# Attention's begin and the quantised FFN: order of splits, scores and product parts; one pass less in each rounding

## The reference, cut to what matters

```python
q2 = (q @ wiq.T + biq).reshape(N, H, D).transpose(1, 0, 2)      # N 384, H 16 heads, D 64
k2 = (k @ wik.T + bik).reshape(N, H, D).transpose(1, 0, 2)
v2 = (v @ wiv.T + biv).reshape(N, H, D).transpose(1, 0, 2)
scores = jnp.einsum('hnd,hmd->hnm', q2, k2) * scale + mask[None]
attn = jax.nn.softmax(scores, axis=-1)
out = jnp.einsum('hnm,hmd->hnd', attn, v2)
...
def act_quant(x):
    scale = 127.0 / jnp.clip(jnp.max(jnp.abs(x), axis=-1, keepdims=True), 1e-05)
    q = jnp.clip(jnp.round(x * scale), -128.0, 127.0) / scale
    return x + jax.lax.stop_gradient(q - x)
def bitlinear(x, w, b):
    xq = act_quant(rmsnorm(x))
    wq = weight_quant(w)
    return jnp.einsum('bsd,fd->bsf', xq, wq) + b
h = bitlinear(x, w1, b1)
h = jax.nn.gelu(h, approximate=False)
return bitlinear(h, w2, b2)
```

## Time and profile before

| | us |
|---|---|
| median of three runs | 803.56 |
| lowest, highest | 803.52, 804.91 |
| profiled execution, its own time | 805.4 |
| span of the profiled execution | 803.7 |

### The profile page before, as it was taken

How to read it: one execution, slowest core, us unless ns; L and a number is a source line. 1 busy time by engine, 2 the same in 40 slices (tenths; PEclk the granted TensorE clock), 3 DMA queues, 4 the chain that set the end, 5 groups by cost and what they waited for, 6 DMA issues and landing times. The chain is left out here.

```text
span 803.7 us, 11529 instructions
## 1 busy us (share of the span) xinstructions
PE 777.5 (97%) x4270; PEld 687.8 (86%) x4270; DVE 586.9 (73%) x1240; ACT 387.0 (48%) x800; POOL 48.7 (6%) x88
## 2 busy tenths in 40 slices
PE   5999999999999899999998799999999999999998
PEld 5888878889999899998876488888888879999886
DVE  8988888645554788998689968889896677675331
ACT  5222123444443576775676647574673343454220
POOL 3000000000000000101102211000002020000000
PEclk9999999999999999999999999999999999999999
DMA  5522124432334322319965349234135135334331
GB/s 188 184 80 79 53 70 141 130 114 97 116 121 150 100 73 73 118 29 332 270 235 144 104 117 279 91 105 157 53 107 144 55 121 146 130 132 154 122 130 39
DMA packets 28775, 102.17 MB, mean 127 GB/s; under 512 B 3736, under 2 KB 3864, under 8 KB 28464
## 3 DMA queue, kind: packets, MB, share of 16 engines
q1 hardware_dynamic: 24784, 86.76, 32.1%
q0 software_dynamic: 3936, 14.68, 8.3%
HBM read 91.99 MB, written 1.57 MB: 116 GB/s over the span
## 5 line engine op out<-in xcount | busy, mean ns | idle before, releaser
L1197 DVE TENSOR_TENSOR w_lo<-raw,w_hi 128x1024 fp32r<-128x1024 f32 x140 | 169.7, 1221 | 64.9 <-ACT w_hi L907 64.5
L907 ACT ACTIVATE w_hi<-raw 128x1024 fp32r<-128x1024 f32 x140 | 147.3, 1057 | 105.9 <-PE bank L1983 79.6
L1931 PE MATMUL bank<-xn1T,w_hi 128*128 128x384 f32 x416 | 106.8, 337 | 0.0
L1983 PE MATMUL bank<-w_hi,xn3T 128*128 128x512 f32 x288 | 92.1, 393 | 0.0
L1931 PEld LDWEIGHTS bank<-xn1T,w_hi 128*128 128x128 f32 x416 | 74.3, 188 | 0.9 <-issue 0.3
L1931 PE MATMUL bank<-xn1T,w_lo 128*128 128x384 f32 x208 | 69.6, 335 | 0.0
L1983 PEld LDWEIGHTS bank<-w_hi,xn3T 128*128 128x128 f32 x288 | 54.1, 188 | 11.0
L1931 PE MATMUL bank<-xn4T,w_hi 128*128 128x384 f32 x240 | 61.2, 335 | 0.0
L1983 PE MATMUL bank<-w_lo,xn3T 128*128 128x512 f32 x144 | 56.0, 389 | 0.0
L1931 PEld LDWEIGHTS bank<-xn4T,w_hi 128*128 128x128 f32 x240 | 43.2, 188 | 0.0
L1931 PE MATMUL bank<-xn4T,w_lo 128*128 128x384 f32 x120 | 40.2, 335 | 0.0
(11 more groups left out here) (363 smaller groups left out, 1717.2 us busy)
## 6 DMA issues: line engine op xcount, KB each, us to landing
raw<-weights SPq DMA_DIRECT2D x140, 512.0 KB, 3.3
row_sb<-rows SPq DMA_DIRECT2D x6, 512.0 KB, 5.9
kcat<-kcat POOLq DMA_DIRECT2D x16, 192.0 KB, 2.8
base<-rows POOLq DMA_DIRECT2D x6, 512.0 KB, 13.2
w2r<-w_in SPq DMA_DIRECT2D x1, 2048.0 KB, 9.8
w1r<-w_in POOLq DMA_DIRECT2D x1, 2048.0 KB, 9.2
x_sb<-x_in SPq DMA_DIRECT2D x3, 512.0 KB, 4.6
row_sb<-rows SPq DMA_DIRECT2D x6, 256.0 KB, 4.8
```

The source lines that it names most:

```text
L907: act.activation(w_hi[:, u % RING], raw[:, u % RAW], ACT.Copy).then_inc(hi_split, 1)
L1197: dve.tensor_tensor(w_lo[:, u % RING], raw[:, u % RAW], f(w_hi[:, u % RING]), ALU.subtract).then_inc(unit_split, 1)
L1931: last = pe.matmul(out_of(pr)[:, 0:N], w[pa][:, slot, k * P:(k + 1) * P], TT[src][:, pb, k], start=(k == 0 and m == 0), stop=(k == KD - 1 ...
L1983: last = pe.matmul(out_of(pr)[:], tile[:, pa, k, ts], w[pb][:, at_, j * HALF:(j + 1) * HALF], start=(kk == 0 and j == 0 and m == 0 and nam ...
```

## The change

Five edits:

1. The weight split that stood right behind the evacuation of k chunk 1 (unit k2.1 plus 3, which is k chunk 2) is moved behind `probs` 0, on ACT and on DVE.
2. In the order of ACT and DVE, `scores` 2 is moved ahead of the evacuation of q chunk 2 and of the weight split that belongs to it. The step in front of it in STEPS is q chunk 2, and TensorE keeps that order.
3. The third transposed tile of head 1, `pT.1.2`, goes to bank 7 in place of bank 1.
4. In `attend` TensorE multiplies v2 high and v2 low by `probT` high for the three tiles first, each behind a wait for ACT's copy alone, and then v2 high by `probT` low for the three tiles, each behind the wait for that tile's bank. The number of matmuls is nine as before.
5. `in_round` and `h_round` do one DVE pass in place of two; the clamps to -128 and 127 are left out. The scale of a row is 127 over the largest magnitude of the row.

```diff
@@ evacuation_order
+    n = steps.index(("scores", 2))
+    steps[n - 1], steps[n] = steps[n], steps[n - 1]
     return steps
@@ plan_banks
-                product(f"pT.{s[1]}.{m}", ((4, 5, 1 if s[1] else 7) if s[1] < H0 - 4 else (1, 4, 5) if s[1] < H0 - 3 else (4, 2, 5))[m])
+                product(f"pT.{s[1]}.{m}", ((4, 5, 1 if s[1] > 1 else 7) if s[1] < H0 - 4 else (1, 4, 5) if s[1] < H0 - 3 else (4, 2, 5))[m])
@@ scalar
-                        if (name, i) == ("k2", 1):
-                            split_up_to(u + AHEAD)
...
                     for m in range(NT):
                         hi_part(probT[:, 0, m], out_of(f"pT.{h}.{m}")[:, 0:N], f"pT.{h}.{m}")
+                    if h == 0:
+                        split_up_to(UNIT_OF[("k2", 1)] + AHEAD)
@@ vector
-                        if (name, i) == ("k2", 1):
-                            split_up_to(u + AHEAD)
...
                         lo_part(probT[:, 1, m], out_of(f"pT.{h}.{m}")[:, 0:N], probT[:, 0, m], f"pT.{h}.{m}")
+                    if h == 0:
+                        split_up_to(UNIT_OF[("k2", 1)] + AHEAD)
...
-                    link(dve.tensor_scalar(xn2[:, t], xn2[:, t], ROUND, ROUND + 127.0, ALU.add, ALU.min))
-                    dve.tensor_scalar(xq[:, t], xn2[:, t], ROUND - 128.0, ROUND, ALU.max, ALU.subtract).then_inc(in_quant, 1)
+                    dve.tensor_scalar(xq[:, t], xn2[:, t], ROUND, ROUND, ALU.add, ALU.subtract).then_inc(in_quant, 1)
...
-                    link(dve.tensor_scalar(hn[:, t], hn[:, t], h_s[:, 5, t:t + 1], ROUND, ALU.mult, ALU.add))
-                    dve.tensor_scalar(hn[:, t], hn[:, t], ROUND + 127.0, ROUND - 128.0, ALU.min, ALU.max).then_inc(h_rounded, 1)
+                    dve.tensor_scalar(hn[:, t], hn[:, t], h_s[:, 5, t:t + 1], ROUND, ALU.mult, ALU.add).then_inc(h_rounded, 1)
@@ tensor, attend
-                    wait_emptied(pe, f"pT.{h}.2")
-                    wait_emptied(pe, f"pT.{h}.1")
-                    wait_emptied(pe, f"pT.{h}.0")
                     wait_bank(pe, pr)
                     js = slice(h // 2 * P, (h // 2 + 1) * P)
-                    full(products(out_of(pr)[:, 0:N], [(lambda p, m=m: v2[:, p, m, js], lambda p, m=m: probT[:, p, m])
-                                                       for m in range(NT)]), pr)
+
+                    for m in range(NT):
+                        pe.wait_ge(act_hi, hi_at[f"pT.{h}.{m}"])
+                        for part in (HI, LO):
+                            pe.matmul(out_of(pr)[:, 0:N], v2[:, part, m, js], probT[:, HI, m], start=(m == 0 and part == HI), stop=False)
+                    for m in range(NT):
+                        wait_emptied(pe, f"pT.{h}.{m}")
+                        last = pe.matmul(out_of(pr)[:, 0:N], v2[:, HI, m, js], probT[:, LO, m], start=False, stop=(m == NT - 1))
+                    full(last, pr)
```

## The result

| | before | after |
|---|---|---|
| median of five runs each, us | 803.56 | 799.61 |
| lowest, highest, us | 803.26, 805.10 | 798.65, 800.38 |
| profiled execution, its own time and span, us | 805.4, 803.7 | 800.38, 798.6 |

The ratio of the times is 0.9944 (95% interval 0.9932 to 0.9956), a gain of 4.4 us by the means of the five. Forecast was a median of 798.1 in a range of 796.7 to 800.6; the median lies inside the range and 1.5 us above the forecast. The forecast for the profiled execution, 799.9, is 0.5 us off.

A forecast was written before the change was run, and what follows sets the result against it. TensorE, busy 777.5 of 803.7 us, was taken as the bound, so only its waits counted. Attention 3.7 plus FFN 1.8 made 5.5 us, taken from the median 803.56: 798.1 us, range 796.7 to 800.6.

The forecast's parts named there:

- The split: Attention's begin: with the weight split later, head 0's product starts 1.67 us earlier and TensorE's wait shrinks to about 0.8 us.
- High parts first: Attention products: worth nothing, since the first matmul waits for bank 7 until VectorE's last low part is done.
- rival (e): Attention products: waits inside the product show as gaps in 16 heads, 14.4 us slower, 812.5 us; chance 0.05.
- Scores and bank 7: Attention's begin: head 2's earlier scores and removed gaps put TensorE 4.2 us ahead; VectorE's chain cuts this to 3.7.
- The FFN: Quantised FFN: one-pass roundings start the second tile's output product 1.8 us earlier; half-clock stretch stays; ends 1.3 and 2.5.
- rival (d): FFN: the clock stays up, so the gain there is 2.5 us, giving 797.4 us; chance 0.12.
- The row and the rule: Input rounding: removed pass priced at 0.71 us from its trace row; the skill page's rule would give 0.61.
- The clock: Attention's begin: the half-clock dip behind the probT wait goes; ten matmuls ran in it, 1.5 us.
- The median: Whole kernel: the 5.5 us gain was taken from the runs' median of 803.56, giving 798.1 us.
- Rival (a): Attention's begin: the clock still falls, head 2's scores come 1.5 us later, 1.6 us lost, 799.7 us; chance 0.08.
- (b): Attention: VectorE takes more back than laid out, 1.7 of 3.7 us stays, 800.1 us; chance 0.10.
- (c): FFN: hidden layer's saving hides behind GELU and squares on ACT, 0.5 instead of 1.1, 798.7 to 799.0 us; chance 0.08.

The follow-up runs named there:

- bank6: Changed kernel with head 0's third transposed tile in bank 6 in place of bank 7; median 799.04 us, ratio 0.9931 to the kernel before.
- rounding_only: Kernel before with only the roundings of input and hidden layer done in one pass in place of two; median 803.04 us, ratio 0.9979.
- before_again: Kernel before, run once more without any edit; median 804.86 us, ratio 1.0002.
- attention_only: Changed kernel with the two passes of each rounding put back; median 801.77 us, ratio 0.9965 to the kernel before.
- the filled wait: Kernel before with ten more matmuls where TensorE waits for head 0's probT; median 803.80 us, ratio 0.9993.
- after_clock_kept_both: Changed kernel with extra matmuls filling TensorE's waits ahead of attend 0 and in the FFN part; median 799.15 us, ratio 0.9931 to the kernel before.
- scores_only: Kernel before with only head 2's scores moved ahead of q chunk 2 and head 1's third transposed tile in bank 7; median 803.60 us, ratio 0.9995.
- after_again: Changed kernel, run once more without any edit; median 799.30 us, ratio 0.9935 to the kernel before.

## Why the prediction was right, and where it was off

**The split.** Product 1.67 us earlier forecast; 1.66 in the kernel with this edit alone. The exponentials, the reciprocal and the second `qcat` stayed where they were, as laid out. Right.

**High parts first.** Nothing forecast. With edit 4 left out nothing changes, and with bank 6, which lets it act, the wait only moves. Right. The rival (e), gaps from waits inside the product (812.5), is refuted by 0.99 + 0.53 us for nine loads, against 1.52 of before.

**Scores and bank 7.** TensorE 4.2 us ahead, cut to 3.7 by VectorE's chain, was the forecast; `kcat` at 285.75, read 285.94, and 3.82 us less from k chunk 1 to 2. That VectorE takes a lead back is shown by `bank6`, where TensorE's 0.8 us are gone at once, and by the changed kernel's new waits behind k chunk 2, 0.36 us and 0.22 more at head 5, which fit the cut of 0.5. Right in the size and in the bound. What the forecast did not say is how much hangs on the bank: it counted 1.1 us of gaps for edits 2 and 3 together, while leaving edit 3 out of the changed kernel costs 4.3.

**The FFN.** 1.8 us forecast; 2.01 us between the two profiles and in `rounding_only` (1.43 behind `ffn_h`, 0.58 ahead of it), 1.7 us in its runs. Right, and 0.2 us too low. Where the forecast held tile 0's saving to be mostly hidden, 0.58 us of it reached TensorE; it does not add to the later tiles' savings but comes before them: counted from the first transposes, those of tile 1 and tile 2 are 0.73 and 0.79 us ahead, forecast 0.71 and 0.74. Of the stretch there the forecast said that it stays and that its absence would be worth 0.7 us more (2.5 for 1.8, rival (d)); 0.8 is measured, but it is absent in one execution and present in another of the same kernel. So (d) is no other way for the kernel to go but something that single executions do.

**The row and the rule.** The removed pass of the input was priced at 0.71 us, from its row; the rule that a semaphore between chained operations costs nothing extra would have given 0.61. It saved 1.32 - 0.60 = 0.72 us, so the trace goes with the row. The rule is that of the Trainium skill, page VectorE: DVE Perf Modes, section The DRAIN you can't avoid; a price by it is 0.1 us a pass too low here. The rule itself is not tested by this, since what follows the two passes is not the same operation.

**The clock, the term that failed.** The size, 1.5 us, is right: 21.19 - 19.63 = 1.56. Wrong was to take it as a property of the kernel before, from one profiled execution. `before_again` has the same wait and no stretch, and so has `rounding_only`. The mean gain of `attention_only`, 2.8 us, is 2.26 and a third of 1.56; the mean gain of the filled wait, 0.6 us, is four tenths of it (its interval, -0.2 to 1.3 us, allows none to eight tenths). So in the mean the term is some 0.6 us, not 1.5, with a wide margin. The runs' own clocks agree: the 14 runs of before at 1.000 lie 1.0 us below the mean of all 73, and the five of `after_clock_kept_both`, all at 1.000, 0.4 us below the changed kernel's ten. So all stretches together cost about 1.0 us before and 0.4 after, 0.6 less.

**The median, the step that joined both.** The profiled execution of before (805.4) had both stretches and lay 1.8 us above the median of three runs (803.56). The forecast took 5.5 us, a gain which holds a stretch of 1.5, from that median, in which by its time such a stretch was hardly there (no trace shows that run). Without it: 803.56 - (5.5 - 1.5) = 799.56, against 799.61. Told by means instead: before 804.4 over 73 runs, after 799.5 over the ten of both sets, 4.9 us; the terms give 2.26 + 2.0 + 0.6 = 4.9, and at full clock 803.4 - 799.1 = 4.3 for 2.26 + 2.0. The median of three, 803.56, was itself 1.0 us below the median of the 73. So the 1.5 us of the miss are about 0.9 for a low base and about 0.6 for the gain.

**The profiled execution.** It was forecast without these two errors, since it is taken from an execution with both stretches. The places of the change gave 3.82 + 2.01 = 5.83 us for 5.5. But the span is only 5.1 us shorter: the changed execution came to `kcat` of k chunk 1 0.33 us later, took 0.29 longer from `kcat` of k chunk 2 to the `w1q` wait (127.94 for 127.65) and 0.14 longer behind the product. The last is the stretch, which lies later against the product now; the first two lie outside the places that were to gain, and they differ as much between other profiles. So the miss of only 0.5 us holds some luck: the places gave more than forecast, and the rest gave part of it back.

Rival (a) would have given 799.7, next to the result, and is false all the same, so the time alone would have chosen the wrong account: the wait is 0.79 us and none of the profiles with edits 1 to 3 has a stretch between 270 and 278. (b), VectorE taking back 2 of 3.7, is false too: 3.82 us in the trace. (c) is false by `rounding_only`.

What stays open: what decides in which executions the clock falls behind a wait of 2.0 to 2.5 us. The traces show that it can fall, that it did behind 3.6 and 3.3 us (one profile each), and that at the attention's begin it did in none of the profiles in which the wait there was shorter than 1 us or filled. In the FFN part equal waits went either way. Edit 3 without edit 2 was not run, so what the bank is worth in the old order stays open too.

## What to carry to other kernels

Before a term from the granted clock goes into a forecast, look at a second profiled execution of the same kernel: a gain that rests on a dip must be taken from a time that has the dip, and a median from few runs may have none. Where an evacuation is moved later in one engine's order, look for the product that reuses its bank on another: here the new order without the new bank costs 4.3 us, and the kernel falls back to 0.9992 of before's time although its other edits stay. A wait taken off the tensor engine can show up again one step later, as the 0.8 us of `bank6` did, so ask first for the pace of the engine that it waits for next.

## What was not expected of the hardware

- The clock fell to 1.2 GHz for 3.4 us behind a wait of 2.48 us in one execution and stayed at 2.4 GHz behind the same wait in three others (`before_again`, `scores_only`, `rounding_only`). The same place cost 1.56 us or nothing.
- It also fell once behind a wait of 2.03 us in the middle of the program (`bank6`, at 415), where the wait is 1.55 or 1.56 us in twelve other profiles and 1.70 in one, and none fell.
- In the FFN part the clock fell in one profile of the changed kernel and stayed up in the other (`after_again`), behind waits that are equal to 0.01 us.
- A stretch at half the clock in the FFN part cost 0.3 to 0.9 us of the 1.2 to 1.7 by which its 16 loads are longer (348.09 to 348.61 us to the end, for 347.71 to 347.78 without one), since the transposes behind them wait for ACT at full clock.
